# Running the convolution and state space of the first batch ahead of its attention, in a fused adaLN block of Mamba, attention and mixture of LoRA experts

## What is computed

```python
h  = layernorm(x) * (1 + ca) + sa
xn = ln(h, ln1_w, ln1_b)
q, k, v = xn @ q_w + q_b, xn @ k_w + k_b, xn @ v_w + v_b        # 16 heads of 16
attn_out = softmax(causal(q k^T / 4)) v @ o_w + o_b
x_ssm, z = split(xn @ in_proj_w)                                 # 512 channels each
x_c = silu(causal_conv4(x_ssm) + conv_b)
x_dbc = x_c @ x_proj_w                                           # 16 + 16 + 16
dt = softplus(x_dbc[:, :16] @ dt_w + dt_b);  Bm, Cm = x_dbc[:, 16:32], x_dbc[:, 32:]
state = exp(dt * A) * state + (x_c * dt) * Bm;  y = sum_n(Cm * state)      # scan over 512 tokens
ssm_out = ((y + x_c * D_param) * silu(z)) @ ssm_out_w
h = h + alpha * attn_out + (1 - alpha) * ssm_out;  h = h + gelu(ffn(ln2(h)))
x = x + ga * h
x = x + gb * (linear + top-2-of-8 LoRA experts)(layernorm(x) * (1 + cb) + sb)
```

## Time and profile before

| what | value |
|---|---|
| median of three runs | 5200.33 us |
| profiled execution, its own time | 5201.05 us |
| its span on the core | 5199.2 us |
| mean granted clock of TensorE | 0.989 of full speed |
| PE busy | 4974.5 us, 96% of the span |
| DVE busy | 4751.3 us, 91% |
| POOL busy | 4629.3 us, 89% |
| ACT busy | 4016.0 us, 77% |
| chain that ended last | PE 71%, DVE 10%, issue 8%, POOL 6%, DMA 2% |

### The profile page before, as it was taken

How to read it: one execution, slowest core, us unless ns; L and a number is a source line. 1 busy time by engine, 2 the same in 40 slices (tenths; PEclk the granted TensorE clock), 3 DMA queues, 4 the chain that set the end, 5 groups by cost and what they waited for, 6 DMA issues and landing times.

```text
span 5199.2 us, 94534 instructions
## 1 busy us (share of the span) xinstructions
PE 4974.5 (96%) x32280; PEld 3447.1 (66%) x32280; DVE 4751.3 (91%) x7332; ACT 4016.0 (77%) x6403; POOL 4629.3 (89%) x2925
## 2 busy tenths in 40 slices
PE   5899999999999999999999999999999999999997
PEld 2567666667666667666677667677666676666665
DVE  4999999999999999999999999999999999999984
ACT  4777887877887877877877878878878778878773
POOL 4899999999999999999999999999999999999983
PEclk7999999999999999999999999999999999999998
DMA  5555555554555554555555555545555555555541
GB/s 150 159 152 154 158 166 160 163 156 154 163 161 164 159 163 148 164 167 158 160 153 159 167 167 160 156 152 159 170 161 158 155 155 162 160 164 159 161 141 55
DMA packets 522016, 812.29 MB, mean 156 GB/s; under 512 B 80976, under 2 KB 227832, under 8 KB 521536
## 3 DMA queue, kind: packets, MB, share of 16 engines
q1 hardware_dynamic: 516768, 805.96, 51.2%
q10 hardware_dynamic: 4768, 0.28, 0.1%
HBM read 716.57 MB, written 88.38 MB: 155 GB/s over the span
## 4 chain that ended last, share of the span: by engine, by line
PE 71%; DVE 10%; issue 8%; POOL 6%; DMA 2%; ACT 1%; SPq 1%; DVEq 0%; POOLq 0%; ACTq 0%
PE pY L984 12%; PE pM L1133 9%; PE pM L1145 8%; PE pM L1026 4%; PE pM L1120 4%; PE pM L1060 4%; DVE pD L1262 4%; PE pM L1073 4%; PE pM L993 4%; PE pM L1006 3%; POOL state L600 3%; PE pM L1093 3%; PE pM L1034 2%; PE pM L1117 2%; PE pM L1041 2%
## 5 line engine op out<-in xcount | busy, mean ns | idle before, releaser
L600 POOL TENSOR_TENSOR state<-scan_in,bc 128x1024 f32<-128x1024 f32 x1024 | 2406.7, 2363 | 145.4 <-PE pY L984 136.5
L745 ACT ACTIVATE pD<-scan_in,A 128x512 f32<-128x512 f32 x2048 | 1404.4, 690 | 401.5 <-DVE state L1270 315.9
L1262 DVE TENSOR_TENSOR_SCAN pD<-pD,state 128x512 f32<-128x512 f32 x1280 | 1545.2, 1219 | 69.0 <-ACT pD L745 67.7
L984 PE MATMUL pY<-ident,state 128*128 128x128 f32 x8192 | 1153.2, 275 | 32.4 <-POOL state L588 25.0
L588 POOL TENSOR_TENSOR state<-state,bc 128x512 f32<-128x512 f32 x768 | 969.6, 1274 | 155.8 <-DVE state L1262 155.8
L984 PEld LDWEIGHTS pY<-ident,state 128*128 128x128 f32 x8192 | 907.9, 142 | 267.8 <-issue 108.7
L1301 DVE TENSOR_REDUCE mx<-pM 128x1 f32<-128x512 f32 (+3 forms) x1408 | 860.1, 630 | 154.7 <-PE pM L1075 146.7
L1262 DVE TENSOR_TENSOR_SCAN state<-pD,state 128x512 f32<-128x512 f32 x768 | 916.4, 1210 | 57.7 <-ACT pD L745 57.6
L846 ACT ACTIVATE region<-pM 128x512 f32<-128x512 f32 (+1 forms) x1408 | 741.7, 559 | 177.8 <-PE pM L1095 153.9
L1270 DVE TENSOR_TENSOR state<-pD,bc 128x512 f32<-128x512 f32 x1280 | 862.1, 680 | 11.0
L1073 PE MATMUL pM<-region 96*128 96x512 bf16 (+3 forms) x2048 | 521.4, 301 | 24.8 <-DVE region L1318 12.1
(11 more groups left out here) (172 smaller groups left out, 8068.1 us busy)
## 6 DMA issues: line engine op xcount, KB each, us to landing
bc<-bc_d SPq DMA_DIRECT2D x2048, 256.0 KB, 3.9
region<-qk_d SPq DMA_DIRECT2D x640, 128.0 KB, 3.7
qk_d<-qkp SPq DMA_DIRECT2D x64, 384.0 KB, 3.4
qk_d<-ht SPq DMA_DIRECT2D x64, 384.0 KB, 5.1
xt<-in_x_dram SPq DMA_DIRECT2D x32, 512.0 KB, 5.4
hres_d<-xt SPq DMA_DIRECT2D x32, 512.0 KB, 4.4
region<-qk_d SPq DMA_DIRECT2D x256, 64.0 KB, 3.1
x<-hres_d SPq DMA_DIRECT2D x32, 512.0 KB, 5.2
```

Source lines behind the costliest of these rows:

```text
L600: nc.gpsimd.tensor_tensor(state[:, at_:at_ + JP], us[:, parity(b), k // N * JP:(k // N + 1) * JP, :], bc[:, k % BC_SLOTS, 0, :].unsqueeze( ...
L745: act.activation(pD[DECAY_BANK[e]][:], dts[:, parity(b), j], ACT.Exp, scale=A[:, j, n:n + 1]).then_inc(a_ok.sem, 1)
L984: ins = pe.matmul(y_part(t, e % JP), state[:, e % RING, t * P:(t + 1) * P], ident[:], is_transpose=True, start=False, stop=(e % PASS >= PA ...
L1262: v.tensor_tensor_scan(h if e in POOL_C else decay, decay, h, 0.0, ALU.mult, ALU.add)\
```

## The change

The opening (all steps of batch 0 that come before the first turn, and the first turn itself) gets an order of its own. Each engine first does the steps of a new list, EARLY, for batch 0, and then what is left of the opening in its old order. From the second turn on nothing is different.

- PE: xt0 xt1, then xs0 to xs3, then qk0 qk1 qk2, then xp, dt0 to dt3, and qk3 last. Before it was qk0 xs0 qk1 xs1 qk2 qk3 xs2 xs3 xp dt0 to dt3.
- DVE: the convolution, then scan0 c0 scan1 scan2 c1 c2 scan3, and only then the row maxima mx0_0 to mx0_3, which stood ahead of scan0.
- POOL: qr3 and ql3 move behind u0 and fill0, and u1 behind fill1.
- ACT: qk3 stands behind the softplus and the first decay, qm3 behind the second, and dec2 and dec3 ahead of the evacuation of v.
- SP: the write of x_dbc and the rows rb0 rc0 rb1 rc1 move ahead of the write of qk3 and of ld0. l1a (the write of the residual) moves behind ld0.
- In batch 0 the full values of the four query and key steps go into four tiles of their own (qk_first), in a part of region that attention uses later, so that the waits on dbc fall away there. Two waits are added for batch 0: PE's xs0 for both transposed activations, SP's first row of B for the write of x_dbc.

```diff
@@ -229,6 +229,7 @@
             Ks.append(view(G * L // 2, BF16).rearrange("p (h t) -> p h t", h=G))
         probs = [view(G * n).rearrange("p (h t) -> p h t", h=G) for n in (L, L - P)]
         shared = at[0]
+        qk_first = region[:, shared:shared + 4 * L].rearrange("p (n t) -> p n t", n=4)
         oT = view(L)
         otok = view(TB * D).rearrange("p (t f) -> p t f", t=TB)
         aoT = view(KT * L).rearrange("p (k t) -> p k t", k=KT)
@@ -354,21 +355,28 @@
 
         block = ctx.enter_context(nc.Block())
 
-        def drive(eng, order, step, banks=()):
+        def drive(eng, order, step, early, banks=()):
 
             def turn(b, first, last):
                 for name, shift in order:
                     if not (first and shift < 0 or last and shift > 0):
                         step(name, b.next(shift))
 
-            for name, shift in order:
-                if shift > 0:
-                    step(name, Batch(None, 0))
-            for n in range(B):
-                turn(Batch(None, n), n == 0, n == B - 1)
+            opening = [(name, 0) for name, shift in order if shift > 0]
+            opening += [(name, shift) for name, shift in order if shift >= 0]
+            for name in early:
+                opening.remove((name, 0))
+            for name, n in [(name, 0) for name in early] + opening:
+                step(name, Batch(None, n))
+            for n in range(1, B):
+                turn(Batch(None, n), False, n == B - 1)
             for name, shift in order:
                 if shift < 0:
                     step(name, Batch(None, B - 1))
+
+        def residual_of(b, n):
+
+            return qk_first[:, n] if b.off == 0 else qkf[:]
 
         def router_parts():
 
@@ -442,6 +450,8 @@
 
             def bc_row(b, k, row):
 
+                if b.off == 0 and k == 0 and row == 0:
+                    b.wait(sp, bc_out)
                 slot = k % BC_SLOTS
 
                 before, last = (b, k - BC_SLOTS) if k >= BC_SLOTS else (b.next(-1), k - BC_SLOTS + UNITS)
@@ -529,7 +539,7 @@
                     b.wait(sp, o_fin)
                     sp.dma_start(out[b.index].rearrange("(t p) f -> p t f", p=P), nrm(b)).then_inc(out_done.sem, 16)
 
-            drive(sp, ORDER["SP"], step)
+            drive(sp, ORDER["SP"], step, EARLY["SP"])
             sp.wait_ge(out_done.sem, 16 * B)
             sp.wait_ge(hres_out.sem, 16 * B)
             for n in range(2):
@@ -627,11 +637,11 @@
                 elif name[:2] == "qr":
                     n = int(name[2])
                     b.wait(pool, qk_f, n + 1)
-                    nc.gpsimd.tensor_tensor(qkf[:], qkf[:], qk_parts[n % 2][:, 0], ALU.subtract).then_inc(qk_r.sem, 1)
+                    nc.gpsimd.tensor_tensor(residual_of(b, n), residual_of(b, n), qk_parts[n % 2][:, 0], ALU.subtract).then_inc(qk_r.sem, 1)
                 elif name[:2] == "ql":
                     n = int(name[2])
                     b.wait(pool, qk_mid, n + 1)
-                    nc.gpsimd.tensor_tensor(qk_parts[n % 2][:, 2], qkf[:], qk_parts[n % 2][:, 1], ALU.subtract)\
+                    nc.gpsimd.tensor_tensor(qk_parts[n % 2][:, 2], residual_of(b, n), qk_parts[n % 2][:, 1], ALU.subtract)\
                       .then_inc(qk_lo.sem, 1)
                 elif name in ("u0", "u1"):
 
@@ -782,17 +792,17 @@
                         b.wait_last(act, qk_out[n % 2])
                     act.activation(qk_parts[n % 2][:, 0], pM[bank_of(name)][:], ACT.Identity,
                                    bias=qkv_b[:, n // 2, n % 2:n % 2 + 1]).then_inc(qk_hi.sem, 1)
-                    if n:
+                    if n and b.off:
                         b.wait(act, qk_lo, n)
-                    else:
+                    elif b.off:
                         b.wait_last(act, dt_ps)
                         b.wait_last(act, bc_out)
-                    act.activation(qkf[:], pM[bank_of(name)][:], ACT.Identity,
+                    act.activation(residual_of(b, n), pM[bank_of(name)][:], ACT.Identity,
                                    bias=qkv_b[:, n // 2, n % 2:n % 2 + 1]).then_inc(qk_f.sem, 1)
                 elif name[:2] == "qm":
                     n = int(name[2])
                     b.wait(act, qk_r, n + 1)
-                    act.activation(qk_parts[n % 2][:, 1], qkf[:], ACT.Copy).then_inc(qk_mid.sem, 1)
+                    act.activation(qk_parts[n % 2][:, 1], residual_of(b, n), ACT.Copy).then_inc(qk_mid.sem, 1)
                 elif name[0] == "v":
                     n = int(name[1])
                     b.wait(act, v_ps, n + 1)
@@ -811,7 +821,8 @@
                     act.activation(xc[:], xc[:], ACT.Silu).then_inc(xc_ok.sem, 1)
                 elif name == "xp":
                     b.wait(act, xp_ps)
-                    b.wait(act, qk_lo)
+                    if b.off:
+                        b.wait(act, qk_lo)
                     act.activation(dbc[:], pM[bank_of(name)][:], ACT.Copy).then_inc(xp_ok.sem, 1)
                 elif name[:2] == "dt":
                     j = int(name[2])
@@ -1036,6 +1047,8 @@
                     ins.then_inc(v_ps.sem, 1)
                 elif name in ("xs0", "xs1", "xs2", "xs3"):
                     j = int(name[2])
+                    if j == 0 and b.off == 0:
+                        b.wait(pe, xt_ok)
                     ps = next_bank(name, b, xs_c, 3 * j + 3)
                     for k in range(KT):
                         ins = pe.matmul(ps[:], w_in[:, k, j * P:(j + 1) * P], xnT[:, k],
@@ -1480,6 +1493,13 @@
         +mx0_6 +c9 +scan10 +scan11 +c10 +mx0_7 +scan12 +mx0_8 +scan13 +c12
     """,
 }.items()}
+EARLY = {engine: text.split() for engine, text in {
+    "SP": "load qk0 qk1 xp qk2 rb0 rc0 rb1 rc1 qk3 ld0 l1a",
+    "POOL": "l0s l0a l0b l0c l1s qr0 ql0 qr1 ql1 qr2 ql2 u0 fill0 qr3 ql3 fill1 u1",
+    "ACT": "l0a l1a xt0 xt1 xs0 xs1 xs2 xs3 qk0 xsilu qm0 qk1 qm1 qk2 xp dt0 dt1 qm2 dt2 dt3 sp2 dec0 qk3 dec1 qm3 dec2 dec3",
+    "PE": "xt0 xt1 xs0 xs1 xs2 xs3 qk0 qk1 qk2 xp dt0 dt1 dt2 dt3 qk3",
+    "DVE": "l0s l1s xs0 xs1 xs2 xs3 scan0 c0 scan1 scan2 c1 c2 scan3",
+}.items()}
 PLACE = {}
 PLACE.update((name, 0) for name in """
     f2_1 mx1_3 mx1_6 st0_0_1 mx1_8 h3t0 st0_1_1 mt1 st0_1_3 axt out0 mx2_3 st0_3_0 mx2_8 st1_0_3 st1_1_1 st1_1_3
```

More of the change, by code:

```diff
@@ L680, in _ @@
             pool.wait_ge(built, BUILT)
-            drive(pool, ORDER["POOL"], step)
+            drive(pool, ORDER["POOL"], step, EARLY["POOL"])
         @block.scalar
@@ L911, in step @@
                     act.activation(axT(b), pM[bank_of(name)][:], ACT.Copy).then_inc(axt_ok.sem, 1)
-            drive(act, ORDER["ACT"], step)
+            drive(act, ORDER["ACT"], step, EARLY["ACT"])
         @block.tensor
@@ L1177, in step @@
                     ins.then_inc(out_ps.sem, 1)
-            drive(pe, ORDER["PE"], step, banks)
+            drive(pe, ORDER["PE"], step, EARLY["PE"], banks)
         @block.vector
@@ L1400, in step @@
                         ins.then_inc(o_fin.sem, 1)
-            drive(dve, ORDER["DVE"], step)
+            drive(dve, ORDER["DVE"], step, EARLY["DVE"])
 MAX_FILLS = ([(3, [h]) for h in range(G)] + [(2, [h]) for h in range(G)]
```

## The result

The kernel after takes 5209.06 us in the median of 20 runs (5203.59 to 5215.71), the kernel before, on the same chips, 5201.20 us (5195.83 to 5203.62, 20 runs). The ratio is 1.0016, with a 95% interval from 1.0010 to 1.0023. So it is 7.9 us slower. The interval doesn't reach 1, so a difference of this size can be told from none, though it is under the 0.2% that the prediction took for the bound of what can be told. The profiled execution took 5210.45 us, 9.4 us more than that of before.

A forecast was written before the change was run, and what follows sets the result against it. From the first scan on, DVE's place in its list was taken as the opening's clock. First scores +10.4 less 0.4 gave +10.0 us at mx0_4: 5201.05 + 10.0 = 5211.05 profiled, 0.72 above the median, so 5210.3; range 5200 to 5216.

The forecast's parts named there:

- Up to x_dbc: Opening up to dt0 on PE: silu ends at 68.1 and dt0 starts at 74.45, 7.9 us early.
- From dt0 to scan0: Opening from dt0 to DVE's first scan: scan0 starts at 88.0 instead of 96.14, 8.1 us earlier.
- I take the second, as 2.6 is nearer to 3.22: PE's 2.6 us gap ahead of dt0: assumed 1.2 GHz behind it, charging 2.0 us for matmuls of dt0 and dt1.
- the forecast's case: Whole opening, with the low clock behind PE's gap ahead of dt0: 5210.3 us; chance 0.40.
- the rival in which the clock stays up: PE ahead of dt0: clock stays up, all from dt0 on is 2.0 us earlier, 5208.3 us; chance 0.22.
- The 0.4 us taken off for the add of c2: Between mx0_0 and mx0_4: c2's add may have waited there before; 0.4 us taken off, bounds 0 and 1.
- From scan0 to the maxima: From fill0's end to first scores: 5.64 us to ld0 at 93.6, then 6.54; mx0_0 at 100.15, 10.4 us later.
- The sign: DVE after scan0: its longest wait, some 6 us, released by PE's scores, those by a DMA of qk_d near 100.
- From there on all lists are the same and each engine waits for the same others, so it stays: From mx0_4 to the end: the +10.0 us delay stays, with the same 10 us one, ten and thirty batches on.
- the rival in which the opening absorbs the delay: DVE's idle time from 96.1 to 180 us takes away 6.4 of 10.0 us: +3.6, 5203.9 us; chance 0.17.
- The faster rival: DVE's queue at mx0_0: ld0 by some 88.5 keeps scan0's lead of 8.1 us, 5192.2 us; chance 0.11.
- The drain that was weighed: ACT's silu table load: a drain of about 1.38 us would make silu 1.4 later, the sum 11.4, 5211.7 us.

The follow-up runs named there:

- experiment 4: Changed kernel with SP issuing rb2 and rb3 ahead of the write of qk3 and ld0: 5207.07 us, ratio 1.0009 to the kernel before.
- experiment 8: The changed kernel itself, unedited, run again beside the others on the same chip: 5212.13 us, ratio 1.0020 to the kernel before.
- Experiment 9: Changed kernel with the wait for ld0 filled by rows, scans, decays and PE work moved on SP, PE, ACT, DVE: 5197.97 us, ratio 0.9998 to the kernel before.
- experiment 1: Changed kernel with v0, v1, z0, skip0 and add0 to add2 ahead of mx0_0 on PE, ACT to match: 5204.04 us, ratio 1.0007 to the kernel before.
- experiment 2: Changed kernel with the four scans behind the maxima again, ACT to match: 5207.48 us, ratio 1.0012 to the kernel before.
- experiment 3: Changed kernel with POOL's qr3 and ql3 behind fill1 and u1, a longer way to ld0: 5213.23 us, ratio 1.0026 to the kernel before.
- experiment 5: Changed kernel with SP, POOL and PE in the old order, only the scans ahead of the maxima, ACT to match: 5213.14 us, ratio 1.0019 to the kernel before.
- experiment 6: Changed kernel with v0 in PE's gap ahead of dt0 and qk3, qm3, qr3, ql3 earlier: 5209.56 us, ratio 1.0015 to the kernel before.
- experiment 7: Changed kernel with v0 ahead of dt0, qk3's steps and rb2, rb3 earlier, v1, z0 ahead of mx0_0: 5205.64 us, ratio 1.0010 to the kernel before.

## Why the prediction was right

**The result** (5209.06) lies 1.2 us under the forecast of 5210.3 and inside its range. Part of that closeness is luck: the forecast was counted from a median of three runs, 5200.33, and the kernel before takes 5201.20 in the median of 20. As a difference, +10.0 was forecast and +7.9 measured. In the trace, the sum said +10.0 us at mx0_4, and 8.13 were measured.

**Up to x_dbc.** Silu's end was forecast for 68.1 and came at 67.4; dt0 for 74.45 and came at 73.60. Of that, 0.35 is the setup, which ended earlier (46.31 against 46.66), and 0.3 the convolution of xs1, which ran at 53.71 and not in the old slot of 54.34. The wait of qk2 for the DMA of qk0's parts was there: 0.8 us for ACT. With qk2's two evacuations and the copy of x_dbc behind it, PE stood 2.2 us ahead of dt0.

**From dt0 to scan0.** This is the term that was mis-sized. The step "I take the second, as 2.6 is nearer to 3.22" charged 2.0 us for a low clock behind the gap. From dt0 to u0 the kernel before took 6.77 us and the changed one 7.71 (73.60 to 81.31): 0.94 us were paid, and not in the matmuls that I had named. The granted clock in stretches from 71.3 to 80 us:

```profile
71.30:73.60 2.30, 0.08 (x2) 0.01 (x1) 0.00 (x0) 1.75 (x3) 1.37 (x2) 1.00 0.21 70
73.60:76.00 2.40, 1.98 (x6) 0.73 (x6) 0.00 (x0) 1.25 (x3) 0.69 (x1) 0.99 0.50 155
76.00:80.00 4.00, 3.93 (x5) 1.40 (x6) 0.00 (x0) 2.92 (x5) 1.15 (x1) 0.50 0.35 100
```

It was 1.00 through the gap and 0.99 for the six matmuls of dt0 to dt2, and 0.50, which is 1.2 GHz, from dt3 on. Neither the forecast's case nor the rival in which the clock stays up is exactly this; it lies between them. The totals can't tell their 5210.3 and 5208.3 apart. The same 7.71 or 7.72 us were taken in experiments 4, 8 and 9. In experiments 1, 2 and 3 it was 8.66, 8.32 and 8.19 us, with the same gap of 2.2 us and the same list up to there. So the price differs from one execution to the next, 0.9 to 1.9 us, all inside the bound of 0 to 2.0.
With that, the sum closes: 10.0, less 0.85 up to dt0, less 1.06 for the clock, is 8.1, and 8.13 were measured. The 0.4 us taken off for the add of c2 fit by chance. From mx0_0 to mx0_4 the changed kernel takes 0.3 us less (12.80 against 13.11): the adds gained 0.5 (1.47 against 1.98 us), the scores and v0 ahead of them lost as much. What is left is on DVE: in the kernel before, the scores of mx0_4 were there 0.3 us before DVE was done with scan3, and in the changed kernel DVE waits for them. The row of B cost nothing: fill0 started at u0's end.

**From scan0 to the maxima.** The chain was forecast at 5.64 us from fill0's end to ld0 and measured at 5.67 (86.03 to 91.70), and from ld0 to the first scores 6.54 us against 6.47. PE's new wait stands where it was said to, released by the DMA of qk_d. DVE's is split otherwise than forecast. The sign was its longest wait, some 6 us, ahead of the first maxima. It measured 3.65 there, since the scores came 2 us earlier than forecast, and the four scans took 9.1 us (86.18 to 95.27) and not 7, with 2.2 of waiting for fill1, which the prediction had not counted. The longest, 6.21, stands ahead of mx0_4, behind v1, z0, skip0 and the adds. Experiments 1, 3, 4 and 9 show that the late ld0, with the work that stands behind the scores, is what counts, and not POOL's row.

**What was covered.** POOL's wait ahead of fill2, 7.8 us, was forecast as covered, and experiment 4 shows it free.

**Does it stay.** This step of the prediction fell short. "From there on all lists are the same and each engine waits for the same others, so it stays" has no loss, and a distance that shrinks after 113 us was named as a sign of being wrong. It did shrink, by 1.4 of 8.2 us. Nor is that one execution: in the seven traces in which mx0_4 is late by 7 us or more (the changed kernel twice, experiments 2 to 6), 1.2 to 1.5 us are lost by batch 1. In experiments 1 and 7, late by 2, it is 0.3 and nothing. So the rival in which the opening absorbs the delay is right in kind and has the size wrong: it had 6.4 us. And what is taken in doesn't grow with the delay, as experiment 3 shows: 5.6 us on top of the changed kernel's were still 5.5 at batch 1.

**The faster rival** needed ld0 at 88.5 and got 91.7. Experiment 9 removes DVE's wait the other way: not by an early ld0, but by enough scans ahead of the scores that are free to run, with their rows, decays and bank users also taken out from behind the scores. The lead of 8.1 us that the rival has at scan0 isn't kept even so: 2.1 are left at scan8. The drain that was weighed, from the Trainium skill, "ScalarE: Activation LUTs", What ACT_TABLE_LOAD costs, is not borne out: silu started at 65.50, right at the end of its table load (64.20 + 1.28), so the trace has no 1.4 us there. Nor is it ahead of the load, which starts as ACT's last step ends (63.51 + 0.68).

## What to carry to other kernels

Work that is moved ahead gains only up to the first step that another queue still holds back. In kernels with hand-written orders, price a reordering at the first point where both orders have the same work behind them, on the engine that is full from there on, and follow the step that was put last through its DMAs: here 10 us won at the first scan turned into 8 us lost at mx0_4. When a transfer must come late, take out from behind its first reader, on every engine, what could have run without it. And a one-time effect of a few microseconds is read from equal steps in two traces. Take off first what was there ahead of the change, as the end of the setup and the clock: two traces of one kernel differ by half a microsecond here, while the totals scatter by ten.

## What was not expected of the hardware

- The granted clock of PE behind a gap of 2.2 us was not settled by the gap. In four executions with the same list and the same gap (the changed kernel twice, experiments 4 and 9) it stayed up for six matmuls and then fell; in experiments 2 and 3 it fell among those six, and in experiment 1 the first of them already ran at 0.50. Filling the gap down to 0.5 us (experiment 6) didn't keep it up: dt3 took 2.07 us there too. In experiment 7, with the gap filled as well, dt3 took 1.12 us and the clock fell one step later, in qk3.
- Turns of the loop are alike to 0.3 us for long stretches (156.8 to 157.1 us), and then single turns take 1 to 3 us more, in places that most executions share (near 2130 and near 3860 us, before and after alike) and in places that they don't: experiment 9 lost 5.7 us near 3000 us. Between the traces compared here, that is where the executions differ most, more than in the opening. Its cause was not looked for and stays open.
